# A second transformer block regrouped as 16 positions x 8 sequences, with its attention on TensorE, behind cross-attention as a phase of its own

## The chip, the cores and the metric

The kernel runs on one core of a Trainium2 chip. The metric is the device time of one execution in microseconds (us). Five engines work side by side, each on a queue of its own in program order: TensorE (PE, with its weight loads shown apart as PEld), VectorE (DVE), ScalarE (ACT), GpSimd (POOL) and SyncE (SP, which only issues DMAs here). They wait for each other through semaphores.

## The reference, cut to what matters

There are 8 sequences of 512 positions with 512 features: 4096 tokens. Cross-attention has 16 heads and reads 77 context rows for each sequence. The second block works **across the 8 sequences at one position**: its hidden states are (S=8, B=512, H=512), so a token attends to the at most 8 tokens with its own position in the sequences up to its own. It has 16 query heads and 4 key-value heads of 32 features.

```python
x = x + xattn(layernorm(x), ctx_1024, ctx_1024, ...)   # 16 heads, 77 keys, causal over (512, 77)
# second block, on layernorm(x) as (8, 512, 512)
ln1 = layer_norm(h, ln1_weight, ln1_bias); qkv = ln1 @ qkv_weight.T
scores = einsum('bgqsd,bgtd->bgqst', qb, kb) * scale   # s, t: the 8 sequences; b: the 512 positions
attn = softmax(where(tril(8, 8), scores, min)); ao = einsum('bgqst,bgtd->bgqsd', attn, vb)
h1 = h + ao @ proj_weight.T
logits = layer_norm(h1, ...) @ router_weight            # 8 experts, top 2, capacity 1280 each
out = x + h1 + moe(...)                                 # experts 512 -> 1024 -> 512, gelu
```

## The kernel before

The program has four parts, each a block of all engines with a barrier at its end: the setup (weights are loaded, two of them transposed on PE, all split into a high and a low half for three-pass products; keys `kT` and values `va` of the context are made), the main part, the routing, and the experts.

The main part handles 32 tiles of 128 tokens. Tile t holds 128 positions of sequence t % 8 (`row0`); chunk t // 8 says which 128 positions. It runs in 40 steps; in step i every stage works on its own tile, named by its lag: load and norm (0), `xt` transposes (1), `q` for two tiles at even steps (2), scores of cross-attention and softmax (2), `pt` transposes of the shares, `pv`, `wo` (3), residual, statistics, `zt` and `qkv` of the second block (4), its attention (5 and 6), `at` and `pj` (7), `z2t` and the router's logits `lg` (8). The lists are written out by hand for each engine, in one order that every step repeats. Four PSUM banks serve as a ring for all PE products in the order of `JOBS`; `bank_free` waits until the bank four jobs back has been read.

The attention of the second block before: POOL multiplies queries by the keys of the sequences so far (`prod_k`, L452) and shares by values (`prod_v`, L469), DVE sums both (L699, L710). Their size grows with the sequence number of the tile: 128 elements times (t % 8 + 1), four times each. So one step in eight is small and one in eight is large. The softmax of cross-attention reads PSUM: DVE adds the mask (L770, tiles under 8), takes the maximum (L773), ACT does 16 exponentials with accumulated sums (L626), DVE multiplies by the reciprocals (L690). `low_half` (L679) makes the low half of a split, for `xT`, `aT` and `oT`.

What PE waits for in one step, in its order: shares, `xT_lo` (q), the query evacuation (scores), `pT` (pv), `zT_lo` (qkv) and `oT_lo` (wo). `wo` comes last, behind 24 matmuls of `qkv`.

## Time and profile before

| | |
|---|---|
| median of 3 runs (lowest to highest) | 1815.31 us (1813.96 to 1817.59) |
| profiled execution, its own time | 1818.26 us |
| its span | 1816.5 us |
| mean granted TensorE clock, of full speed | 0.911 |
| setup, main part, routing, experts | 68, 912, 63, 774 us |

The four parts are read from the trace: the main part runs from 68 to 980 us of the span, the routing to 1043. The page gives busy shares of the whole span (PE 83%, DVE 61%, POOL 54%, ACT 44%), an average over parts with different limits.

### The profile page before, as it was taken

The numbers are of one execution on the slowest core, as the hardware profiler recorded it, in microseconds if no ns is written. First come the engines' busy times: TensorE is split into PE (matmuls) and PEld (weight loads), VectorE is DVE, ScalarE is ACT, GpSimd is POOL, SyncE is SP. The second block draws the span as 40 slices with busy tenths as digits, with TensorE's granted clock in tenths as the row PEclk, the third lists the DMA queues.
The fourth block names the chain that finished last, engine by engine and source line by source line (L and its number), as shares of the span: only waits on it lengthen the run. The fifth ranks groups of instructions, "written<-read, shape, count | busy, mean of one in ns | idle before, by whom it ended". The sixth has DMA issues, their size and how long they took to land. (4 is left out here: it accounts for less than half of the span.)

```text
span 1816.5 us, 31665 instructions
## 1 busy us (share of the span) xinstructions
PE 1513.9 (83%) x10604; PEld 1324.4 (73%) x10605; DVE 1105.9 (61%) x1778; ACT 802.6 (44%) x2385; POOL 975.8 (54%) x925
## 2 busy tenths in 40 slices
PE   7778877799777988789752579999999979999986
PEld 5367766677666776677642478989999968999975
DVE  3256888967897798877866953544333374353361
ACT  2066654565555655457421043544333354343240
POOL 2014676756785677667884254655344385454342
PEclk9879997899898988889875789999999989999999
DMA  7101101111101111111001132433333352433221
GB/s 188 35 18 36 44 28 36 36 49 48 47 24 47 49 36 36 36 36 42 24 35 71 45 109 64 94 95 101 74 71 81 58 128 66 92 94 88 34 37 21
DMA packets 57936, 106.95 MB, mean 59 GB/s; under 512 B 14314, under 2 KB 14314, under 8 KB 57771
## 3 DMA queue, kind: packets, MB, share of 16 engines
q1 hardware_dynamic: 26707, 58.42, 10.1%
q0 software_dynamic: 17920, 29.08, 9.4%
q10 hardware_dynamic: 13144, 17.23, 2.7%
q8 instruction: 106, 1.74, 0.4%
q14 instruction: 59, 0.48, 0.1%
HBM read 79.83 MB, written 37.75 MB: 65 GB/s over the span
## 5 line engine op out<-in xcount | busy, mean ns | idle before, releaser
L1347 PE MATMUL hidden_ps<-gT,w 128*128 128x256 f32 x2880 | 351.8, 284 | 5.4 <-ACT hT L1269 2.5
L1347 PEld LDWEIGHTS hidden_ps<-gT,w 128*128 128x128 f32 x2880 | 349.4, 192 | 9.1 <-ACT hT L1269 5.2
L1376 PE MATMUL expert_ps<-w,hT 128*128 128x512 f32 x1440 | 340.2, 396 | 8.0 <-DVE og L1316 8.0
L1376 PEld LDWEIGHTS expert_ps<-w,hT 128*128 128x128 f32 x1440 | 272.1, 191 | 64.7 <-DVE og L1316 8.5
L1294 DVE TENSOR_TENSOR hT<-gl,hT 128x512 fp32r<-128x512 f32 x160 | 132.0, 834 | 246.9 <-ACT hT L1269 238.8
L1156 POOL TENSOR_TENSOR w<-raw,w 128x1024 fp32r<-128x1024 f32 x64 | 155.3, 2442 | 206.5 <-ACT w L1150 205.6
L1267 ACT ACTIVATE gl<-hidden_ps 128x512 f32<-128x512 f32 x160 | 95.8, 598 | 335.1 <-PE hidden_ps L1347 239.2
L1249 POOL DMA_INDIRECT out_dram<-og,idx x80 | 132.7, 1659 | 155.0 <-DVE og L1316 141.3
L452 POOL TENSOR_TENSOR prod_k<-qb,kc 128x128 f32<-128x128 f32 (+7 forms) x128 | 182.6, 1428 | 30.4 <-ACT vs L652 28.1
L626 ACT ACTIVATE pr<-score_ps,nm 128x77 f32<-128x77 f32 x512 | 158.7, 363 | 78.1 <-DVE nm L776 78.1
L469 POOL TENSOR_TENSOR prod_v<-pa,vc 128x128 f32<-128x128 f32 (+7 forms) x128 | 156.5, 1233 | 24.7 <-DVE ao L710 20.5
L1316 DVE TENSOR_SCALAR og<-expert_ps,shares 128x512 f32<-128x512 f32 x80 | 59.1, 749 | 161.3 <-PE expert_ps L1376 150.8
L710 DVE TENSOR_REDUCE ao<-prod_v 128x128 f32<-128x128 f32 (+7 forms) x128 | 138.5, 1097 | 5.1 <-POOL prod_v L469 5.1
L699 DVE TENSOR_REDUCE sc<-prod_k 128x4 f32<-128x128 f32 (+7 forms) x128 | 95.7, 749 | 55.5 <-POOL prod_k L452 55.5
L1277 ACT ACTIVATE gT<-yk 128x256 fp32r<-128x256 f32 x160 | 67.2, 420 | 139.2 <-DVE yk L1303 135.6
L626 ACT ACTIVATION_READ_ACCUMULATOR pr<-score_ps,nm 128x1 f32 x512 | 125.0, 244 | 0.0
L840 PE MATMUL ring_ps<-ident,pr 128*77 128x128 f32 x512 | 88.1, 328 | 40.5 <-DVE pr L690 37.2
L823 PE MATMUL ring_ps<-ident,ao 128*128 128x128 f32 x128 | 28.4, 363 | 110.9 <-DVE x L724 83.5
L840 PEld LDWEIGHTS ring_ps<-ident,pr 128*77 128x77 f32 x512 | 75.9, 184 | 52.2 <-DVE pr L690 45.6
L1239 POOL DMA_INDIRECT xg<-normed_tokens,idx x80 | 86.7, 1084 | 49.3 <-POOL idx L1234 34.6
L823 PEld LDWEIGHTS ring_ps<-ident,ao 128*128 128x128 f32 x128 | 18.7, 181 | 117.6 <-DVE ao L710 111.1
L1269 ACT ACTIVATE hT<-hidden_ps 128x512 fp32r<-128x512 f32 x160 | 95.6, 598 | 14.8 <-PE expert_ps L1376 14.8
(186 smaller groups left out, 3352.7 us busy)
## 6 DMA issues: line engine op xcount, KB each, us to landing
raw<-L_ffn_moe_w_dram SPq DMA_DIRECT2D x64, 512.0 KB
xa<-x_dram SPq DMA_DIRECT2D x32, 256.0 KB, 2.8
xc<-x_dram SPq DMA_DIRECT2D x32, 256.0 KB, 2.7
out_dram<-x ACTq DMA_DIRECT2D x32, 256.0 KB, 2.0
normed_tokens<-z ACTq DMA_DIRECT2D x32, 256.0 KB, 2.3
xg<-normed_tokens,idx POOLq DMA_INDIRECT x80
out_dram<-og,idx POOLq DMA_INDIRECT x80
cx<-ctx_dram SPq DMA_DIRECT2D x1, 1232.0 KB
```

The costliest lines, as they stand in the source:

```text
L452: pool.tensor_tensor(prod_k[:, g % 2, 0:n * P].rearrange("p (t h d) -> p t h d", t=n, h=HQ), bc(qb[:, t.s % 2, g * P:(g + 1) * P].rearrang ...
L469: pool.tensor_tensor(prod_v[:, g % 2, 0:n * P].rearrange("p (t h d) -> p t h d", t=n, h=HQ), bc(w, 3, shape), bc(vc[:, 0:n, g * DH:(g + 1) ...
L626: e = act.activation(pr[:, b, g, :], psS[:, b, g * SK:(g + 1) * SK], ACT.Exp, bias=nm[:, h:h + 1], scale=SCALE, accum_out=den[:, h:h + 1])
L699: dve.tensor_reduce(sc[:, g * HQ:(g + 1) * HQ, 0:n].rearrange("p h t -> p t h"), prod_k[:, g % 2, 0:n * P].rearrange("p (t h d) -> p t h d ...
L710: dve.tensor_reduce(ao[:, g * P:(g + 1) * P], prod_v[:, g % 2, 0:n * P].rearrange("p (t f) -> p f t", t=n), X, ALU.add).then_inc(s["sums_v ...
L840: last = pe.transpose(bank(i, "pt", b)[0:SK, g * P:(g + 1) * P], pr[:, b, g, :], ident[:, :])
L1156: pool.tensor_tensor(weight_piece(p, 1, j), raw[:, j % 2, :], weight_piece(p, 0, j).bitcast(F32), ALU.subtract).then_inc(s["w_lo"], 1)
L1249: pool.indirect_dma_start(out=out2d[:, :], out_offset=rows(g, k), in_=og[:, k, :], in_offset=None, bounds_check=N - 1, oob_is_err=False, c ...
L1267: act.activation(gl[:, q % 2, :], pH[:, q, :], ACT.Gelu_apprx_tanh)
L1294: dve.tensor_tensor(o[1], gl[:, q % 2, :], o[0].bitcast(F32), ALU.subtract)\
L1347: last = pe.matmul(pH[:, q, f * W:(f + 1) * W], w1[p][l][:, k, cols], xT[g.s % 2][r][:, k, :], start=k == 0 and n == 0, stop=k == KT - 1 a ...
L1376: last = pe.matmul(pY[:, k, :], hT[par][l][:, f, k * P:(k + 1) * P], w2[p][r][:, f, :], start=f == 0 and n == 0, stop=f == FT - 1 and n == 2)
```

## The change

The main part is written anew. Cross-attention keeps its tiles and runs in steps 0 to about 36; its result is written to DRAM (`mid`). The second block reads `mid` back in tiles of another shape, 16 positions of all 8 sequences (`block_rows`: four DMAs of 32 rows, each row 2 KB), and its tile f works in steps 30 + f to 33 + f (`FF` = 30), so that the program has 66 steps in place of 40, written out without a loop. In a tile of the second block, each group of 32 tokens holds 4 positions x 8 sequences. Its attention is done on PE: scores by one matmul that adds the mask and four of 128x128 against a block-diagonal `kbd` (`s2`), four transposes of the shares (`p2t`), four matmuls against `vbd` (`o2`). DVE turns queries, keys and the result in blocks of 32x32 (`dve.transpose`). `prod_k`, `prod_v` and their sums are gone, the `at` transposes too.

In cross-attention, the 16 exponentials with accumulators become a subtraction of the maxima on DVE (2), two exponentials on ACT, two sums on DVE; the multiplication by the reciprocals goes from DVE to POOL, and `pt`, `pv` and `wo` come one step later (`LP` = 4). The residual is added at lag 5.

The weights and the context come from the host already laid out and transposed, and so do the constants, so the setup's PE transposes and POOL's constants are gone. The routing loads six constants by DMA and adds a third prefix product (`lower_seq`), since a tile's tokens are no longer in order. The experts are as before.

```diff
+TB = 32
+FX = 6
...
+    mid = nc.dram_tensor("attended_rows", [N, D], F32, kind="Internal").ap()
...
-JOBS = [("pt", 3, 0), ("pt", 3, 1), ("xt", 1, 0), ("at", 7, 0), ("pt", 3, 2), ("pt", 3, 3), ("q", 2, 0), ("q", 2, 1),
-        ("z2t", 8, 0), ("zt", 4, 0), ("pj", 7, 0), ("pv", 3, 0), ("lg", 8, 0), ("qkv", 4, 0), ("qkv", 4, 1),
-        ("wo", 3, 0)]
+LP = 4
+FF = NT - 2
+STEPS = NT + FF + 4
...
+def ring_jobs(i):
+    tx, tq, tp = tile(i, 1), tile(i, 2), tile(i, LP)
+    fz, fs, fo, fr = (tile(i, FF + n) for n in range(4))
+    jobs = [("pt", tp, 0), ("pt", tp, 1), ("xt", tx, 0), ("pt", tp, 2), ("pt", tp, 3), ("zt", fz, 0), ("o2", fo, 0)]
+    if i % 2 == 0:
+        jobs += [("q", tq, 0), ("q", tq, 1)]
+    jobs += [("s2", fs, 0), ("pv", tp, 0), ("z2t", fr, 0), ("pj", fo, 0), ("p2t", fs, 0), ("qkv", fz, 0),
+             ("lg", fr, 0), ("qkv", fz, 1), ("wo", tp, 0)]
+    return [job for job in jobs if job[1] is not None]
...
+        jobs = [("k", m, h) for m in range(KT) for h in range(2)] + [("v", b, 0) for b in range(S)]
...
+                    for n in range(2):
+                        sp.wait_ge(x2_out[n], 16 * 4 * (f // 8 + 1))
+                    need(sp, base_out[f % FX], 64 * (f // FX))
+                    for j in range(4):
+                        sp.dma_start(fx[TB * j:TB * (j + 1), f % FX, :], block_rows(mid, f, j))\
+                          .then_inc(fx_in[f % FX], 16)
...
-                    pool.tensor_tensor(prod_k[:, g % 2, 0:n * P].rearrange("p (t h d) -> p t h d", t=n, h=HQ),
-                                       bc(qb[:, t.s % 2, g * P:(g + 1) * P].rearrange("p (h d) -> p h d", h=HQ),
-                                          1, shape),
-                                       bc(kc[:, 0:n, g * DH:(g + 1) * DH], 2, shape), ALU.mult)\
-                        .then_inc(s["prods_k"], 1)
...
+                t = tile(i, LP - 1)
+                if t is not None:
+                    for half in range(2):
+                        pool.wait_ge(s["rec_done"], 2 * t + half + 1)
+                        shares = pr[:, t % 2, 2 * half:2 * half + 2, :, :].rearrange("p b g k -> p (b g) k")
+                        pool.tensor_tensor(shares, shares, bc(rec[:, t % 2, 8 * half:8 * half + 8], 2, [P, 8, SK]),
+                                           ALU.mult).then_inc(s["shared"], 1)
...
+                if f is not None:
+                    pool.wait_ge(s["rec2_done"], f + 1)
+                    pool.tensor_tensor(p2[:, f % 2, :, :], p2[:, f % 2, :, :], bc(rec2[:, f % 2, :], 2, [P, 16, TB]),
+                                       ALU.mult).then_inc(s["shared2"], 1)
...
+                f = tile(i, FF - 1)
+                if f is not None:
+                    pool.wait_ge(s["stat_f"], f + 1)
+                    var = mvf[:, f % 2, 1:2]
+                    link(pool, "pool_link", linked,
+                         pool.tensor_scalar(wf[:, 0:1], var, 1.0 + EPS, EPS * EPS, ALU.mult, ALU.add))
+                    pool.tensor_tensor(rff[:, f % 2:f % 2 + 1], wf[:, 0:1], expo[:, 0:1], ALU.pow)\
                         .then_inc(s["rstd_f"], 1)
...
+                    need(pool, s["h0_done"], f - 3)
+                    link(pool, "pool_link", linked, power(rf[:, f % 4:f % 4 + 1], var, wf[:, 1:2]))
+                    pool.tensor_scalar(shift[:, f % 4:f % 4 + 1], mvf[:, f % 2, 0:1], rf[:, f % 4:f % 4 + 1], -1.0,
+                                       ALU.mult, ALU.mult).then_inc(s["shift_f"], 1)
+                f = tile(i, FF + 2)
+                if f is not None:
+                    pool.wait_ge(s["stat_h"], f + 1)
+                    power(rh[:, f % 2:f % 2 + 1], mvh[:, f % 2, 1:2], wh[:, :]).then_inc(s["rstd_h"], 1)
+                    pool.tensor_tensor(fx[:, f % FX, :], fx[:, f % FX, :], h1[:, f % 2, :], ALU.add)\
                         .then_inc(s["base_done"], 1)
...
-                                               bias=nm[:, h:h + 1], scale=SCALE, accum_out=den[:, h:h + 1])
-                        e.then_inc(s["exp_done"], 1)
-                t = At(c, i - 5)
...
+                if t is not None:
+                    for half in range(2):
+                        act.wait_ge(s["shifted"], 2 * t + half + 1)
+                        shares = pr[:, t % 2, 2 * half:2 * half + 2, :, :]
+                        act.activation(shares, shares, ACT.Exp, scale=SCALE).then_inc(s["exp_done"], 1)
...
+                f = tile(i, FF + 1)
+                if f is not None:
+                    dve.wait_ge(s["qkv_mm"], 2 * f + 1)
+                    need(dve, s["s2_mm"], f)
+                    dve.transpose(hq[:, :, :], parts(bank("qkv", f, 0))).then_inc(s["q_turned"], 1)
+                    dve.wait_ge(s["v_kept"], f + 1)
+                    for j in range(4):
+                        rows = slice(TB * j, TB * (j + 1))
+                        k_turn = dve.transpose(kbd[rows, :, j, :],
+                                               bank("qkv", f, 1)[rows, 0:P].rearrange("p (g d) -> p g d", g=NKV))
+                    k_turn.then_inc(s["k_turned"], 1)
...
+                if f is not None:
+                    dve.wait_ge(s["o2_mm"], f + 1)
+                    need(dve, s["a_lo"], f)
+                    dve.transpose(ao[:, :], bank("o2", f)).then_inc(s["ao_done"], 1)
...
+                    dve.wait_ge(s["a_hi"], f + 1)
+                    dve.tensor_tensor(aT[1][:, :, :], parts(ao[:, :]), aT[0][:, :, :].bitcast(F32),
+                                      ALU.subtract).then_inc(s["a_lo"], 1)
...
+                    dve.wait_ge(s["s2_mm"], f + 1)
+                    scores = bank("s2", f).rearrange("p (b k) -> p b k", b=16)
+                    need(dve, s["p2t_mm"], f - 1)
+                    chained(dve.tensor_reduce(nm2[:, :], scores, X, ALU.max, negate=True))
+                    dve.tensor_tensor(p2[:, f % 2, :, :], scores, bc(nm2[:, :], 2, [P, 16, TB]), ALU.add)\
+                       .then_inc(s["s2_sub"], 1)
...
+                    chained(dve.tensor_reduce(nm[:, :].rearrange("p (b g) -> p b g", b=4), scores, X, ALU.max,
+                                              negate=True))
+                    need(dve, s["pt_mm"], 4 * (t - 1))
+                    for half in range(2):
+                        dve.tensor_tensor(pr[:, t % 2, 2 * half:2 * half + 2, :, :],
+                                          scores[:, 2 * half:2 * half + 2, :, :],
+                                          bc(nm[:, 8 * half:8 * half + 8].rearrange("p (b g) -> p b g", b=2), 3,
+                                             [P, 2, 4, SK]), ALU.add).then_inc(s["shifted"], 1)
...
+                    dve.wait_ge(s["o_hi"], t + 1)
+                    dve.tensor_tensor(oT[1][:, :, :], parts(bank("pv", t)), oT[0][:, :, :].bitcast(F32),
+                                      ALU.subtract).then_inc(s["o_lo"], 1)
...
+                    dve.wait_ge(s["exp2"], f + 1)
+                    need(dve, s["shared2"], f - 1)
+                    chained(dve.tensor_reduce(den2[:, :], p2[:, f % 2, :, :], X, ALU.add))
+                    dve.reciprocal(rec2[:, f % 2, :], den2[:, :]).then_inc(s["rec2_done"], 1)
...
+                    dve.wait_ge(s["h0_done"], f + 1)
+                    dve.wait_ge(s["pj_mm"], f + 1)
+                    dve.tensor_tensor(h1[:, f % 2, :], bank("pj", f), h1[:, f % 2, :], ALU.add)\
+                       .then_inc(s["h1_done"], 1)
+                    dve.wait_ge(s["h1_done"], f + 1)
+                    stats(h1[:, f % 2, :], bnh, mvh[:, f % 2, :]).then_inc(s["stat_h"], 1)
...
+                    dve.wait_ge(fx_in[f % FX], 64 * (f // FX + 1))
+                    need(dve, s["shift_f"], f - 1)
+                    stats(fx[:, f % FX, :], bnf, mvf[:, f % 2, :]).then_inc(s["stat_f"], 1)
...
+                    for half in range(2):
+                        heads = slice(8 * half, 8 * half + 8)
+                        dve.wait_ge(s["exp_done"], 2 * t + half + 1)
+                        shares = pr[:, t % 2, 2 * half:2 * half + 2, :, :].rearrange("p b g k -> p (b g) k")
+                        chained(dve.tensor_reduce(den[:, heads], shares, X, ALU.add))
...
+                    dve.wait_ge(s["rstd_h"], f + 1)
+                    need(dve, z2_out[f % 2], 64 * (f // 2))
+                    need(dve, s["z2t_mm"], f - 1)
+                    dve.tensor_scalar(z2[:, f % 2, :], h1[:, f % 2, :], mvh[:, f % 2, 0:1], rh[:, f % 2:f % 2 + 1],
+                                      ALU.subtract, ALU.mult).then_inc(s["z2_done"], 1)
...
+                    dve.wait_ge(s["rstd_f"], f + 1)
+                    need(dve, s["zt_mm"], f)
+                    dve.tensor_scalar(z[:, :], fx[:, f % FX, :], mvf[:, f % 2, 0:1], rff[:, f % 2:f % 2 + 1],
...
+                if tp is not None:
+                    turn_shares(tp, (0, 1))
+                if tx is not None:
+                    pe.wait_ge(s["normed_x"], tx + 1)
+                    transposes("xt", tx, xa[:, tx % 3, :]).then_inc(s["xt_mm"], 1)
+                if tp is not None:
+                    turn_shares(tp, (2, 3))
+                if fz is not None:
+                    pe.wait_ge(s["z_done"], fz + 1)
+                    transposes("zt", fz, z[:, :]).then_inc(s["zt_mm"], 1)
+                if fo is not None:
+                    pe.wait_ge(s["p2t_evac"], fo + 1)
+                    pe.wait_ge(s["v_spread"], fo + 1)
+                    bank_free(pe, "o2", fo)
+                    for g in range(NKV):
+                        last = pe.matmul(bank("o2", fo)[:, g * P:(g + 1) * P], p2T[:, g, :],
+                                         vbd[:, fo % 2, g, :, :].rearrange("p j d -> p (j d)"), start=True, stop=True)
+                    last.then_inc(s["o2_mm"], 1)
...
+                if fs is not None:
+                    pe.wait_ge(s["q_turned"], fs + 1)
+                    pe.wait_ge(s["k_turned"], fs + 1)
+                    bank_free(pe, "s2", fs)
+                    pe.matmul(bank("s2", fs), token_sel[:, :], token_mask[:, :], start=True, stop=False)
+                    for g in range(NKV):
+                        last = pe.matmul(bank("s2", fs)[:, g * P:(g + 1) * P], hq[:, g, :],
+                                         kbd[:, g, :, :].rearrange("p j k -> p (j k)"),
+                                         start=False, stop=g == NKV - 1)
+                    last.then_inc(s["s2_mm"], 1)
+                if tq is not None:
+                    pe.wait_ge(s["q_evac"], 4 * (tq // 2) + 4)
...
+                if tp is not None:
+                    pe.wait_ge(s["pt_evac"], 4 * tp + 4)
...
+                if fr is not None:
+                    pe.wait_ge(s["z2_done"], fr + 1)
+                    transposes("z2t", fr, z2[:, fr % 2, :]).then_inc(s["z2t_mm"], 1)
+                if fo is not None:
+                    pe.wait_ge(s["a_lo"], fo + 1)
+                    bank_free(pe, "pj", fo)
+                    split_matmuls(pe, bank("pj", fo), lambda h, k: aT[h][:, k, :], lambda h, k: wpj[h][:, k, :])\
+                        .then_inc(s["pj_mm"], 1)
+                if fs is not None:
+                    pe.wait_ge(s["shared2"], fs + 1)
...
+                if fz is not None:
+                    pe.wait_ge(s["z_lo"], fz + 1)
+                    bank_free(pe, "qkv", fz, 0)
+                if fr is not None:
+                    pe.wait_ge(s["y2_done"], 4 * fr + 4)
+                    bank_free(pe, "lg", fr)
...
+                if tp is not None:
+                    pe.wait_ge(s["o_lo"], tp + 1)
+                    bank_free(pe, "wo", tp)
+                    split_matmuls(pe, bank("wo", tp), lambda h, k: oT[h][:, k, :], lambda h, k: wo[h][:, k, :])\
                         .then_inc(s["wo_mm"], 1)
...
+            for dst, name in ((ranks, "expert_ranks"), (ahead, "ahead_in_tile"), (same_seq, "same_seq"),
+                              (lower_seq, "lower_seq"), (ramp, "ramp"), (number, "token_numbers")):
+                sp.dma_start(dst[:, :], a[name]).then_inc(made, 16)
...
+            dve.tensor_reduce(lower[:, :], pp[:, 2, 0:NT * E].rearrange("p (t e) -> p e t", e=E), X, ALU.add)
...
+            pe.matmul(pp[:, 2, 0:NT * E], lower_seq[:, :], flat, start=True, stop=True).then_inc(prefixed, 1)
```

## Rows read from the trace of the kernel before

**Rows 1.** The windows view: stretch, length, busy by engine, PEclk, DMA share, GB/s.

```profile
97.80:112.60 14.80, 11.87 (x97) 10.03 (x98) 8.43 (x14) 9.80 (x48) 2.03 (x3) 0.62 0.06 19
...
588.74:607.45 18.71, 18.09 (x200) 15.43 (x204) 15.31 (x34) 15.54 (x59) 13.02 (x21) 1.00 0.25 87
716.21:748.30 32.09, 24.94 (x141) 22.25 (x144) 27.65 (x34) 14.22 (x54) 21.92 (x21) 0.84 0.05 18
68.00:980.00 912.00, 710.84 (x5632) 613.39 (x5632) 696.24 (x1070) 492.14 (x1824) 577.73 (x640) 0.87 0.11 38
```

**Rows 2.** The waits of PE, 470 to 800 us: total, times, longest.

```profile
PE ring_ps L823 <- DVE x L724: 42.5, 11, 5.2
```

**Rows 3.** The timeline of step 3, an odd step without the second block.

```profile
97.80 1.99 PE L840 MATMUL ring_ps<-ident,pr 128*77 128x128 f32 x8 [6.94 <-DVE pr L690]
...
102.28 1.13 PE L869 MATMUL score_ps<-kT,qT 32*128 32x77 f32 x32
...
103.34 1.08 PE L880 MATMUL ring_ps<-pT,va 77*32 77x128 f32 x32
...
104.96 1.44 DVE L773 TENSOR_REDUCE nm<-score_ps 128x16 f32<-128x1232 f32 x1
...
106.52 0.68 DVE L679 TENSOR_TENSOR oT_lo<-ring_ps,oT_hi 128x512 fp32r<-128x512 f32 x1
...
107.35 0.77 PE L413 MATMUL ring_ps<-wo_hi,oT_hi 128*128 128x512 f32 x1 [2.93 <-DVE oT_lo L679]
...
112.56 1.03 PE L840 MATMUL ring_ps<-ident,pr 128*77 128x128 f32 x8
```

**Rows 4.** The timeline of steps 4 and 5 on PE: q's ends, wo, scores, shares.

```profile
115.63 0.36 PE L413 MATMUL ring_ps<-xT_hi,wq_hi 128*128 128x256 f32 x1 [0.62 <-DVE xT_lo L679]
...
121.28 0.28 PE L413 MATMUL ring_ps<-xT_hi,wq_lo 128*128 128x256 f32 x1
...
122.49 1.13 PE L869 MATMUL score_ps<-kT,qT 32*128 32x77 f32 x32 [0.49 <-ACT qT L577]
...
131.76 0.39 PE L413 MATMUL ring_ps<-wo_hi,oT_hi 128*128 128x512 f32 x1
...
134.50 1.03 PE L840 MATMUL ring_ps<-ident,pr 128*77 128x128 f32 x8
```

**Rows 5.** Groups of instructions by form, 470 to 800 us: total busy, mean ns.

```profile
L690 DVE TENSOR_TENSOR pr<-pr,rec 128x616 f32<-128x616 f32 x24 | 33.5, 1398 | 0.8
...
L593 ACT ACTIVATE y<-ring_ps,ln1b,ln1w 128x128 f32<-128x128 f32 x48 | 18.2, 464 | 1.7 <-PE ring_ps L823 1.5
...
L509 POOL TENSOR_TENSOR zT_lo<-y,zT_hi 128x512 fp32r<-128x512 f32 x12 | 15.3, 1274 | 22.6 <-ACT zT_hi L598 22.6
...
L806 DVE TENSOR_SCALAR z<-h,mvf,rf 128x512 f32<-128x512 f32 x12 | 14.7, 1229 | 0.0
...
L469 POOL TENSOR_TENSOR prod_v<-pa,vc 128x640 f32<-128x640 f32 x8 | 10.7, 1355 | 0.3 <-DVE ao L710 0.3
...
L724 DVE TENSOR_TENSOR x<-ring_ps,xc 128x512 f32<-128x512 f32 x12 | 8.2, 681 | 2.5 <-issue 2.4
...
L598 ACT ACTIVATE zT_hi<-y 128x512 fp32r<-128x512 f32 x12 | 7.6, 633 | 0.5
L441 POOL TENSOR_TENSOR rc<-wc,expo 128x1 f32<-128x1 f32 x12 | 7.4, 619 | 1.0
```

**Rows 6.** The timeline of the setup.

```profile
15.40 19.26 PE L294 MATMUL setup_ps<-cT,rk 128*128 128x308 f32 x64 [0.66 <-DVE cT L260]
...
34.50 1.91 PE L309 MATMUL setup_ps<-ident,rpj 128*128 128x128 f32 x16
...
36.24 2.95 PE L309 MATMUL setup_ps<-ident,rqkv 128*128 128x128 f32 x24
...
67.08 0.69 DVE L268 TENSOR_TENSOR va<-setup_ps,bv 77x512 f32<-77x512 f32 x1 [2.75 <-PE setup_ps L299]
```

**Rows 7.** DMA issues: bytes of one, us from issue to landing.

```profile
xa<-x_dram SPq DMA_DIRECT2D x32, 256.0 KB, 2.8
```

More of the change, by code:

```diff
@@ L435, in _, with power @@
+            for f in range(NT - FX, NT):
+                sp.wait_ge(base_out[f % FX], 64 * (f // FX + 1))
+            for f in range(NT - 2, NT):
+                sp.wait_ge(z2_out[f % 2], 64 * (f // 2 + 1))
         @block.gpsimd
         def _(pool):
-            def rstd(dst, var, work, chain, count):
-                pool.tensor_scalar(work, var, EPS, None, ALU.add).then_inc(chain, 1)
-                need(pool, chain, count)
+            linked = [0]
+            def power(dst, var, work):
+                link(pool, "pool_link", linked, pool.tensor_scalar(work, var, EPS, None, ALU.add))
@@ L520, in step @@
[L520 to L532 removed]
+                f = tile(i, FF + 1)
@@ new lines, in _ @@
+                f = tile(i, FF + 1)
+                if f is not None:
+                    act.wait_ge(s["p2t_mm"], f + 1)
+                    need(act, s["o2_mm"], f)
+                    act.activation(p2T[:, :, :], parts(bank("p2t", f)), ACT.Copy).then_inc(s["p2t_evac"], 1)
+                f = tile(i, FF + 3)
+                if f is not None:
+                    act.wait_ge(s["lg_mm"], f + 1)
+                    act.activation(logits[:, f, :], bank("lg", f)[:, 0:E], ACT.Copy).then_inc(s["lg_evac"], 1)
@@ L1035, in _ @@
                                    pp[:, 1, 0:NT * E].rearrange("p (t e) -> p t e", e=E), ALU.subtract))
+            link(dve.tensor_tensor(place[:, :, :], place[:, :, :], bc(lower[:, :], 1, shape), ALU.add))
             for k in range(2):
```

923 lines of the change are left out of this document (369 added, 554 removed), and 3 rows, old and new, of the table read_out.

## The prediction, made blind

> **What bounds the kernel now.** I read the windows of the four parts first, then the waits of PE in the middle of the main part, then the timeline of single steps. The main part takes 912 us, 28.5 for each of its 32 tiles, with PE busy for 711 us, DVE for 696 and POOL for 578, at a granted clock of 0.87 [rows 1]. The reader should compare two steps there. The stretch from 588.74 to 607.45 us, from one residual of the second block to the next, is 18.7 us long with PE busy for 18.1 at full clock: where the attention products are short, PE sets the step. The stretch from 716.21 is 32.1 us long, with DVE busy for 27.7 and PE for 24.9: where they are long, DVE and POOL set it. PE then waits, above all for DVE's residual (42.5 us in 11 waits) [rows 2]. So the bound changes with the tile, and the sums leave some 200 us of the main part in which PE does nothing.
>
> **PE's own work after the change.** At full clock 48 q matmuls start in 5.65 + 0.12 = 5.8 us, once for two tiles [rows 4], and 12 matmuls of 512 columns (wo) take 134.50 - 131.76 = 2.75 us, 0.23 each [rows 4]; pj takes the same. qkv is 12 of these and 12 of 256 columns: 2.75 + 1.4 = 4.2. Eight transposes end 1.03 after they start and take about 0.9 of PE [rows 4], so 16 share transposes cost 1.8 and a group of four 0.45. Scores and pv take 1.05 each [rows 3]. Cross-attention is thus 1.8 + 0.45 + 2.9 + 1.05 + 1.05 + 2.75 = 10.0 us for a tile (12.9 at even steps, 7.1 at odd ones). New are true fp32 matmuls of 128 columns: the trace shows such matmuls only at 308 columns, 32 of them in 19.3 us (64 records), which gives 0.25 for 128 [rows 6]; a transpose at 0.11 is the bound below. I take 0.22. s2 is then 4 x 0.22 + 0.23 = 1.1, o2 0.9, p2t 0.45, and a tile of the second block 0.45 (zt) + 0.9 + 1.1 + 0.45 (z2t) + 2.75 + 0.45 + 4.2 + 0.9 (lg, eight short records between the others) = 11.2. Together 21.2 us; before, the same list with at and without s2, o2 and p2t was 19.3. PE gains 2 us of work for a tile.
>
> **What is removed.** POOL's products and DVE's sums go entirely, and with them the long steps. On ACT 16 exponentials with accumulator reads go for two of 616 elements. DVE gives the 616-element multiplications, 1.40 us each on average [rows 5], to POOL (about 1.35, as for 640 elements [rows 5]) and gets two subtractions from PSUM. A subtraction of 616 elements is bounded by 0.68 for 512 and 1.44 for 1232 [rows 3]: 0.8. DVE's residual, which also reads one PSUM and one SBUF operand, has a mean of 0.68 beside a busy POOL [rows 5], so I don't charge the 1.40. The Trainium skill (GPSIMD Engine Reference, section 1, Specifications) says that POOL shares its SBUF interface with DVE instructions that have two SBUF inputs; that agrees with 0.68 against 1.40, and without it the two subtractions would cost 1.2 us more.
>
> No engine but PE has 21 us of work for a tile any more: DVE has some 18, POOL 13. But the two phases no longer lie on top of each other, and each then has only its own work to put into its waits.
>
> **The cross-attention phase.** Take the end of wo as zero. PE does shares and xt to 2.2. At an even step q starts at 3.1 (q's start after the shares is late by 0.62 for `xT_lo` [rows 4]) and ends at 8.8; the query evacuation puts the scores at 9.9 (1.1 after q [rows 4]) to 10.9. Now DVE's order counts: maximum 1.44, two subtractions 1.6, and only then `oT_lo` 0.68 [rows 3], with waits 4.0 in all. pv is done at 12.0, and nothing of the second block is left to put between pv and wo. wo starts at 14.8 after 2.9 of idling. Step 3 of before has just this form: wo waited 2.93 us for `oT_lo` and then took 112.56 - 107.35 = 5.2 us in place of 2.75, at the lower level of the clock (0.62 over that step) [rows 1, 3]. So the even step ends at 19.9. At an odd step the scores come right after the shares but behind DVE's norm, at 3.7; `pT` and pv are done at 4.7, `oT_lo` at 7.3, wo at 12.3. The mean is 16.1 us for 10.0 of work. As a test, step 3, odd and with the mask, took 112.56 - 97.80 = 14.8 [rows 3]; my odd step is 12.3 + 1.5 for the mask = 13.8, and step 3's cold shares and its lack of subtractions nearly cancel. With a warm wo it is 17.5 and 9.9, mean 13.7. POOL's multiplications are made a step ahead and hide.
>
> **The second phase.** Take DVE's last norm `z` as zero; DVE turns queries until 0.7 and keys until 1.7, zt and o2 run beside that, and s2 ends at 2.8. A 32x32 turn on DVE is not in the trace; I bound it by 0.54 and 0.8 for 512 elements and take 0.7 as for a copy from PSUM, and four key turns at 0.2 to 0.3. ACT: y four times 0.38 to 0.46, the high half 0.63 [rows 5], then `aT`'s high half at 2.9 to 3.5; DVE's `a_lo` at 4.25; pj 4.3 to 7.1. DVE goes from `a_lo` to maximum and subtraction (5.7), ACT's exponential (6.4), sum and reciprocal (7.3), POOL's multiplication (1.27 for 512 [rows 5], 8.65), p2t, and qkv with lg from 9.2 to 14.3. Beside this runs the other chain: pj, DVE's h1 and two statistics (9.9), POOL's five small operations and two more, of which three powers at 0.6 [rows 5], to 13.0, DVE's z2 and z. z2 meets POOL's add of 1.27 and costs 1.23 on average, against 0.53 alone [rows 5]. That chain closes at 15.1. PE is idle 4 of 15 us, in gaps of about 1 and 1.6. If pj runs at the lower clock (2.4 more) the chain closes at 17.2, with qkv too at 17.5. I take 16.2 for 11.2 of work. The DMAs hide: SP's 12 issues and the landing (2.8 [rows 7]) take about 8 us and are wanted a step later; uncovered they would be those 8 us once in each step.
>
> The Trainium skill (TensorE: Matmul & The Clock Gate, section HAM oscillation) says that a loop whose every turn has a wait on PE starts each turn's work at half clock. By that rule both phases cost their upper values, and the whole would be near 1970; the trace agrees for wo in step 3, and the middle value of the second phase doubts it.
>
> **The sum**, against the 912 us: first steps up to step 4, 30 (97.80 - 68.00 before [rows 1, 3]); steps 4 to 29, 26 x 16.1 = 419; the mask at six of them, 1.5 each, 9; steps 30 to 35 with both blocks, 21.2 of PE when full, less at their start, with 2 to 3 of waiting, 131; steps 36 to 61, 26 x 16.2 = 421; the last four and the stores, 27. Together 1037, +125. Setup: two groups of transposes, 1.9 + 2.95 [rows 6], and some 2 of context transposes that the loads don't cover go, -7; its end, v's matmuls, stays. Routing: six small loads at 2.8 and their issues [rows 7], one more product, one more link: +5. The experts stay. 1818.3 - 7 + 125 + 5 = 1941 for an execution like the profiled one, which lay 3 us above the median: **1938 us**. With its own bounds (16.1 to 13.7, 16.2 to 15.1 or 17.5, fp32 matmuls and turns at either end, overlap 125 to 146): 1841 to 1990.
>
> **The rivals.** (1) The clock stays up through waits of 1.5 to 3 us: 13.7 and 15.1, 26 x 2.4 + 26 x 1.1 + 6 less, 1841; up to 1880 if half of them do. For it: waits of 0.6 in step 4 left q fast [rows 4]. Against: step 3. Chance 0.20. (2) Faster: the waits for `oT_lo` and `shared2` are filled, because DVE is idle in both phases and PE's sum sets the steps. Both together 21.2 for a tile in place of 32.3, 26 x 11.1 = 289 less, near 1650. It decides below 912 + 2 - 197 = 717 us for the 26 pairs, 27.6 a pair: 4.7 of the 11.1 us of waiting would have to be absent. For it: before, with long lists, PE reached 18.1 of 18.7. Against: the waits are made by the order of DVE's list, not by its load. Chance 0.10 for anything faster. (3) Turns on DVE cost double or the overlap jams: 2 us more in 26 steps and 20 more, above 1990. Chance 0.08. (4) No difference, 0.02. My forecast has 0.60.
>
> 0.2% is about what a measurement of this kernel can tell from no change. Faster 0.10, same 0.02, slower 0.88. The range 1830 to 1990 leaves out the faster cases and (3).
>
> **What would show it.** A main part of about 1040 us with 66 steps; in steps 10 to 28 PE's largest wait at wo for `oT_lo`, near 2.9 and 2.6 us, then 12 matmuls at the lower clock; in steps 36 to 61 waits at pj and p2t, a step of 15 to 17.5 us, PE busy 70 to 75%. The prediction is wrong if wo starts right behind pv, or if these steps are shorter than 13 us.

## The result and the profile after

The changed kernel is slower: 1971.09 us (1969.05 to 1971.91, 4 runs) against 1816.45 us (1813.96 to 1817.73) on the same chip, a ratio of 1.0851 [1.0833, 1.087], or +154.6 us. The forecast was 1938 us, +123, in a range of 1830 to 1990.

The windows view of the kernel after, with the columns of [rows 1]. The first two stretches are an even and an odd step of cross-attention alone, from one end of `wo` to the next; the third is a step with both blocks, the fourth a step of the second block alone; then the whole main part, and two long stretches in which only one block runs.

```profile
393.40:413.10 19.70, 15.46 (x146) 13.57 (x145) 8.76 (x13) 6.22 (x12) 4.43 (x5) 0.83 0.12 41
413.10:426.10 13.00, 9.69 (x98) 7.94 (x97) 8.65 (x13) 4.54 (x8) 4.42 (x5) 0.74 0.20 62
565.00:592.50 27.50, 25.27 (x207) 21.98 (x206) 17.71 (x29) 10.96 (x22) 11.09 (x14) 0.94 0.09 29
849.70:868.00 18.30, 15.58 (x80) 13.34 (x80) 10.52 (x19) 6.58 (x16) 7.00 (x11) 0.82 0.13 43
56.40:1128.94 1072.54, 832.81 (x6176) 700.89 (x6176) 628.94 (x1000) 378.83 (x800) 373.88 (x513) 0.86 0.14 48
100.00:480.00 380.00, 285.67 (x2754) 245.75 (x2753) 205.32 (x303) 122.94 (x229) 99.90 (x113) 0.81 0.14 47
720.00:1050.00 330.00, 265.59 (x1414) 217.91 (x1412) 207.64 (x343) 123.89 (x287) 141.10 (x218) 0.91 0.14 46
```

POOL went from 578 busy microseconds in the main part [rows 1] to 374, as the change has it. Yet the main part grew from 912.0 to 1072.5 us, because a tile now passes through two kinds of step, 16.2 and 17.1 us on average, where it had one of 28.5.

The waits of PE in the two long stretches (total, times, longest), which take the place of [rows 2]; the first three rows are of 100 to 480 us, the others of 720 to 1050:

```profile
PE ring_ps L366 <- DVE oT_lo L652: 76.3, 23, 4.8
PE score_ps L759 <- ACT qT L523: 11.1, 12, 0.9
PE ring_ps L366 <- DVE xT_lo L609: 6.9, 11, 0.6
...
PE ring_ps L701 <- DVE z L693: 38.9, 19, 3.0
PE ring_ps L783 <- POOL p L455: 13.9, 13, 1.1
PE ring_ps L366 <- DVE aT_lo L624: 9.4, 13, 1.0
```

Now the timeline of the end of the even step above (start, duration, engine, line), which answers to [rows 3]:

```profile
403.32 1.13 PE L759 MATMUL score_ps<-kT,qT 32*128 32x77 f32 x32 [0.93 <-ACT qT L523]
...
404.38 1.08 PE L768 MATMUL ring_ps<-pT,va 77*32 77x128 f32 x32
404.52 1.44 DVE L641 TENSOR_REDUCE nm<-score_ps 128x16 f32<-128x1232 f32 x1 [6.91 <-PE score_ps L759]
405.53 0.60 ACT L541 ACTIVATE oT_hi<-ring_ps 128x512 fp32r<-128x512 f32 x1 [2.26 <-PE ring_ps L768]
405.99 1.50 DVE L645 TENSOR_TENSOR pr<-score_ps,nm 128x616 f32<-128x616 f32 x2
...
407.42 0.68 DVE L652 TENSOR_TENSOR oT_lo<-ring_ps,oT_hi 128x512 fp32r<-128x512 f32 x1
...
408.15 0.80 PE L366 MATMUL ring_ps<-wo_hi,oT_hi 128*128 128x512 f32 x1 [2.69 <-DVE oT_lo L652]
...
413.08 0.60 PE L709 MATMUL ring_ps<-ident,pr 128*77 128x128 f32 x4
```

`oT_lo` needs nothing but `oT_hi`, which ACT has made by 406.13. It starts at 407.42, behind the two subtractions of the softmax. Then the 12 matmuls of `wo` take 413.08 - 408.15 = 4.9 us, not the 2.75 of [rows 4].

The timeline of a step of the second block alone, from POOL's power operation for `rh` to `pj`:

```profile
860.35 0.57 POOL L422 TENSOR_TENSOR rh<-wh,expo 128x1 f32<-128x1 f32 x1
...
860.87 1.27 POOL L477 TENSOR_TENSOR fx<-fx,h 128x512 f32<-128x512 f32 x1
860.95 1.48 DVE L687 TENSOR_SCALAR z<-h,mvh,rh 128x512 f32<-128x512 f32 x1 [3.23 <-POOL rh L422]
...
862.09 1.23 POOL L442 TENSOR_TENSOR vbd<-vn,blocks 128x512 f32<-128x512 f32 x1
862.35 1.26 DVE L693 TENSOR_SCALAR z<-fx,mvf,rff 128x512 f32<-128x512 f32 x1
...
863.52 0.70 DVE L587 STREAM_TRANSPOSE hq<-ring_ps 128x512 f32<-128x512 f32 x1
863.66 1.11 PE L701 MATMUL ring_ps<-ident,z 128*128 128x128 f32 x4 [2.65 <-DVE z L693]
864.16 1.25 DVE L591 STREAM_TRANSPOSE kbd<-ring_ps 32x128 f32<-32x128 f32 x4
...
868.92 0.50 PE L366 MATMUL ring_ps<-wpj_hi,aT_hi 128*128 128x512 f32 x1 [0.42 <-DVE aT_lo L624]
```

Read the two norms `z` (L687 is `z2`, L693 the first norm of the tile that comes next) against POOL's two operations. POOL's end at 862.14 and 863.32, the norms at 862.43 and 863.61: each norm ends 0.29 us after the POOL operation beside it. The input of L693 has long been there, its `rff` came at 858.6; it stands behind `z2` in DVE's list, and `z2` waits for `rh`. PE stands still for 2.65 us.

Outside the steps, these rows of the setup's timeline and of the DMA issues answer to [rows 6, 7]:

```profile
8.97 18.95 PE L272 MATMUL setup_ps<-cT,rk 128*128 128x308 f32 x64 [8.97 <-DMA rk<-wk_rows_dram]
27.76 27.63 PE L277 MATMUL setup_ps<-rv,cT 128*77 128x512 f32 x64
...
xa<-x_dram SPq DMA_DIRECT2D x32, 256.0 KB, 2.7
```

The keys' products start at 8.97 us in place of 15.40, and the main part at 56.40 in place of 68.05. So +153.3 us of span (1969.8 - 1816.5) are -11.7 for the setup, +160.5 for the main part and +4.5 for what follows (routing 3.4, experts 1.1).

### The profile page after: what moved, and what is told of

Its sections match the earlier page's. It is cut to its first block and busy times, and to the rows that moved or that the text cites. A ratio compares the mean times of both kernels' runs of the same rounds, so it can differ in the third digit from the quotient of the medians.

```text
span 1969.8 us, 30370 instructions
## 1 busy us (share of the span) xinstructions
PE 1626.7 (83%) x11078; PEld 1403.7 (71%) x11079; DVE 1031.4 (52%) x1692; ACT 689.0 (35%) x1353; POOL 768.3 (39%) x785
## 5 line engine op out<-in xcount | busy, mean ns | idle before, releaser
L431 POOL TENSOR_TENSOR pr<-pr,rec 128x616 f32<-128x616 f32 x64 | 77.2, 1227 | 243.2 <-DVE rec L681 243.2
L366 PE MATMUL ring_ps<-wo_hi,oT_hi 128*128 128x512 f32 x128 | 76.7, 599 | 85.4 <-DVE oT_lo L652 85.4
L486 ACT ACTIVATE pT<-ring_ps 77x512 f32<-77x512 f32 x128 | 68.6, 593 | 159.1 <-PE ring_ps L709 159.1
L366 PEld LDWEIGHTS ring_ps<-wo_hi,oT_hi 128*128 128x128 f32 x128 | 36.8, 287 | 100.3 <-DVE oT_lo L652 92.4
L1158 ACT ACTIVATE hT<-hidden_ps 128x512 fp32r<-128x512 f32 x160 | 95.5, 597 | 14.6 <-PE expert_ps L1265 14.6
L687 DVE TENSOR_SCALAR z<-h,mvh,rh 128x512 f32<-128x512 f32 x32 | 47.7, 1489 | 93.2 <-POOL rh L422 93.2
L701 PE MATMUL ring_ps<-ident,z 128*128 128x128 f32 x256 | 47.0, 314 | 55.0 <-DVE z L693 51.6
L1192 DVE TENSOR_SCALAR yk<-gather_ps,ln2w,ln2b 128x256 f32<-128x256 f32 x160 | 83.1, 540 | 11.0 <-PE gather_ps L1249 8.1
L641 DVE TENSOR_REDUCE nm<-score_ps 128x16 f32<-128x1232 f32 x32 | 45.9, 1436 | 77.6 <-PE score_ps L759 77.3
L455 POOL TENSOR_TENSOR p<-p,rec 128x512 f32<-128x512 f32 x32 | 33.5, 1047 | 134.8 <-DVE rec L659 134.8
L450 POOL TENSOR_TENSOR zT_lo<-y,zT_hi 128x512 fp32r<-128x512 f32 x32 | 40.8, 1275 | 115.7 <-ACT zT_hi L511 115.7
```

Of the source, the lines that this page charges most:

```text
L366: last = pe.matmul(dst, lhs(l, k), rhs(r, k), start=k == 0 and n == 0, stop=k == KT - 1 and n == 2)
L431: pool.tensor_tensor(shares, shares, bc(rec[:, t % 2, 8 * half:8 * half + 8], 2, [P, 8, SK]), ALU.mult).then_inc(s["shared"], 1)
L486: act.activation(pT[:, j, :, :], bank("pt", t, j)[0:SK, :].rearrange("p (g n) -> p g n", g=4), ACT.Copy).then_inc(s["pt_evac"], 1)
L1158: act.activation(hT[g.s % 2][0][:, 2 * q:2 * q + 2, :].rearrange("p f n -> p (f n)"), pH[:, q, :], ACT.Gelu_apprx_tanh).then_inc(s["gelu"], 1)
L1192: dve.tensor_scalar(yk[:, k % 2, :].rearrange("p (b n) -> p b n", b=GB), pT[:, :, k * P:(k + 1) * P], ln2w[:, k:k + 1], ln2b[:, k:k + 1], ...
```

## The experiments

Beside these runs, the kernel before measured 1816.15, 1814.38, 1816.46 and 1813.82 us, with experiments 1 to 4, 5 to 8, 9 to 11, and 12 in turn. A ratio is always to before. Spacings of steps are taken between successive residuals `x2` or successive `aT_lo` in each trace.

**1. `oT_lo` ahead of the subtractions.** It stands on DVE right behind the maximum; nothing else moves.

```diff
@@ DVE, behind the maximum of a tile of cross-attention
+                low_half_of_o(tile(i, LP))
                 if t is not None:
                     need(dve, s["pt_mm"], 4 * (t - 1))
...
-                t = tile(i, LP)
-                if t is not None:
-                    dve.wait_ge(s["o_hi"], t + 1)
-                    dve.tensor_tensor(oT[1][:, :, :], ...
```

> Edit: on VectorE the low half of oT is made right behind the maximum of the scores, ahead of the two subtractions, in place of behind them. Theory (the wait at wo is made by the order of VectorE's list): wo starts some 2.6 us after the scores in place of 4.0, in each of 32 steps, 32 x 1.5 = 46 us less; if the shorter wait also leaves the clock at its upper level for wo, up to 2.4 us more in each, 115 less in all: 1855 to 1925 us. Rival (the phases are bound by the sum of an engine's work or by something behind wo): no change, 1971.

Measured: 1933.79 us, ratio 1.0644 [1.062, 1.0668], 37 us less. The wait and the window of 100 to 480 us:

```profile
PE ring_ps L366 <- DVE oT_lo L584: 49.5, 25, 3.4
```

```profile
100.00:480.00 380.00, 310.05 (x3062) 266.68 (x3060) 227.38 (x332) 135.90 (x253) 110.57 (x125) 0.84 0.16 53
```

The wait went from 3.3 to 2.0 us each, and a step from 16.2 to 14.7. The order of DVE's list makes this part of the wait; the other 2.0 us stay. The granted clock rose only from 0.81 to 0.84, so what the lower clock costs is still there, and the gain is below what was expected.

**2. The second block 16 steps behind in place of 30** (`FF = 16`), so that 16 steps and not two have both blocks in full.

> Edit: FF = 16 in place of 30, nothing else; 52 steps, 20 of them with both blocks. Theory (each phase alone has nothing to put into its waits; a pair of steps apart costs 16.2 + 17.1 = 33.3 us, a step with both about 23): 14 pairs more lie on top of each other, 14 x 10.3 = 144 us less, 1827 us (1805 to 1860). Rival (the time is lost by the new form of the attention itself: its matmuls, turns and round trip through DRAM): it costs the same wherever it lies, within 20 us of 1971.

Measured: 1855.43 us, ratio 1.0218 [1.0198, 1.0238], 116 us less. A step with both takes 25.3 us, against 16.2 + 17.1 = 33.3 for two apart. One step less of lag thus saves 33.3 - 25.3 = 8.0 us, 14 of them 112. The expectation had a full step at 23; in its place PE waits 29.2 us in 13 waits of 350 to 680 us for POOL's `p`, the shares `p2` (2.2 each).

**3. `z` ahead of `z2` on DVE.**

```diff
@@ DVE, end of a step
+                f = tile(i, FF - 1)
+                if f is not None:
+                    dve.wait_ge(s["rstd_f"], f + 1)
...
+                    dve.tensor_scalar(z[:, :], fx[:, f % FX, :], ...).then_inc(s["z_done"], 1)
                 f = tile(i, FF + 2)
                 if f is not None:
                     dve.wait_ge(s["rstd_h"], f + 1)
...
-                f = tile(i, FF - 1)
-                if f is not None:
-                    dve.wait_ge(s["rstd_f"], f + 1)
...
-                    dve.tensor_scalar(z[:, :], fx[:, f % FX, :], ...).then_inc(s["z_done"], 1)
```

> Edit: at the end of VectorE's step the norm z of the next tile comes ahead of z2. Theory (in the second phase the chain through GpSimd's small operations and VectorE's two norms, each held by a GpSimd add or multiplication beside it, starts the next step late; PE waits 2.05 us a step for z): z comes some 3 us earlier, the turns behind z2 about 1 us earlier: 1.0 us in 30 steps, 1940 us (1925 to 1960). Rival (the chain of pj, softmax and qkv on PE sets the step, z is merely the wait that shows): within 5 us of 1971.

Measured: 1909.22 us, ratio 1.0512 [1.0492, 1.0532], 62 us less, twice what was expected. The window, the waits of PE and the two norms by form, 720 to 1050 us:

```profile
720.00:1050.00 330.00, 278.24 (x1639) 227.46 (x1638) 221.14 (x404) 146.42 (x336) 163.27 (x240) 1.00 0.15 53
```

```profile
PE ring_ps L783 <- POOL p L455: 24.6, 23, 1.1
PE ring_ps L731 <- DVE hq L587: 20.5, 21, 1.1
```

```profile
L693 DVE TENSOR_SCALAR z<-h,mvh,rh 128x512 f32<-128x512 f32 x23 | 34.4, 1497 | 42.0 <-POOL rh L422 42.0
L686 DVE TENSOR_SCALAR z<-fx,mvf,rff 128x512 f32<-128x512 f32 x21 | 11.6, 551 | 19.9 <-POOL rff L467 19.9
```

The step went from 17.1 to 14.6 us and the granted clock from 0.91 to 1.00. The norm `z` (`z<-fx`, L686 here and L693 in the changed kernel) fell from 1.32 us on average to 0.55: it now lies in DVE's wait for `rh`, when POOL has only operations of one element a partition to do. `z2` (`z<-h`) still costs 1.50. The order cost 26 x 2.5 = 65 us in all. Three things went with it, and no run tells them apart: the norm's wait for `rh`, its longer time beside POOL, and the lower clock.

**4. PE's wait filled.** While PE waits for `oT_lo` in a step without the second block, it does 11 useless matmuls of 128 columns into the bank that `wo` then overwrites. They add work and nothing that anyone needs.

```diff
                 if tp is not None:
-                    pe.wait_ge(s["o_lo"], tp + 1)
                     bank_free(pe, "wo", tp)
+                    if fz is None:
+                        for n in range(11):
+                            pe.matmul(bank("wo", tp)[:, 0:P], ident, ident, ...)
+                    pe.wait_ge(s["o_lo"], tp + 1)
```

> Edit: while PE waits for oT's low half in steps without the second block, it multiplies the identity by itself 11 times (2.5 us) into the bank that wo then overwrites. This adds work without use. Theory (the wait costs twice: its own 2.7 us, and wo's 12 matmuls at the lower level of the clock, 5.1 in place of 2.75): the wait stays, the clock stays up, 26 to 28 steps x 2.3 = 62 us less, 1909 us (1895 to 1930). Rival (the lower clock at wo has another cause): no change, or some us more.

Measured: 1920.68 us, ratio 1.0578 [1.0551, 1.0606], 50 us less, with everything of the change in place. The window shows what the clock did:

```profile
100.00:480.00 380.00, 343.63 (x3693) 309.02 (x3692) 235.55 (x347) 141.98 (x265) 115.99 (x135) 0.98 0.17 56
```

The granted clock is 0.98 where it was 0.81, and a step takes 14.3 us in place of 16.2. The useless matmuls hand no data to anyone, so these 2 us a step come from the clock.

**5 and 6. The edits together**: 1 and 3 with the lag left at 30, then all three.

> Edit: oT's low half right behind the maximum and z ahead of z2, together, with FF = 30 as in the changed kernel. Theory (the two waits lie in different phases and are made by the order of VectorE's list): the two gains add, 1971 - 37 - 62 = 1872 us (1865 to 1882), and the kernel stays slower than the one before, since the phases still lie apart. Rival (both edits mend one common cause, such as the clock): less than the sum, 1895 or more.

> Edit: both orders of before and FF = 16. Theory: a step with both blocks is 25.4 us as with FF = 16 alone, and only the 16 steps of each phase that stay alone gain, 1.4 and 2.3 us each: 1855 - 18 - 33 = 1804 us (1795 to 1820), about as fast as the kernel before. Rival (in a step with both blocks the early wait for oT's high half holds VectorE up): 1820 to 1850.

Measured: 1869.95 us, ratio 1.0305 [1.0275, 1.0335], and 1808.14 us, ratio 0.9957 [0.9942, 0.9972]. The first says that even with both orders mended the phases one behind the other lose: 14.61 + 14.55 = 29.2 us for a tile, against 28.5 before. The second is the first version below before, by 0.4%. The lag now saves less, 29.2 - 25.2 = 4.0 us a step, 14 of them 56 (measured 62). The three gains do not add up: a step with both blocks takes 25.3 us in experiment 2 and 25.2 here, so there the two orders gain next to nothing. The waits that 1 and 3 shorten are filled in it by the other block's work.

**7. The softmax of cross-attention as before the change**: 16 exponentials a tile on ACT, with the maximum as bias and collected sums, in place of two subtractions and two sums on DVE. Only this part is undone; the second block stays 30 steps behind.

```diff
@@ DVE
-                    for half in range(2):
-                        dve.tensor_tensor(pr[...], scores[...], bc(nm[...]), ALU.add)
+                    dve.tensor_scalar(nm[:, :], nm[:, :], -SCALE, None, ALU.mult)
...
-                        chained(dve.tensor_reduce(den[:, heads], shares, X, ALU.add))
@@ ACT
-                        act.activation(shares, shares, ACT.Exp, scale=SCALE)
+                        for b in range(2 * half, 2 * half + 2):
+                            for g in range(4):
+                                act.activation(pr[...], psS[...], ACT.Exp, bias=nm[...], scale=SCALE, accum_out=den[...])
```

> Edit: the softmax of cross-attention as before the change (16 exponentials with accumulated sums on ScalarE, no subtractions and no sums on VectorE), all else as in the changed kernel. Theory (what lies on the path is VectorE between the scores and oT's low half): the two subtractions, 1.6 us, go and a small operation of 0.2 comes, so wo starts 1.2 us earlier in 32 steps; ScalarE's 5 us for a tile hide: 1933 us (1920 to 1945). Rival (this part of the change is its gain, since ScalarE is relieved): slower than 1971, 1985 or more.

Measured: 1933.89 us, ratio 1.0651 [1.0623, 1.0679], 37 us less and the same as experiment 1: `oT_lo` now has no subtractions ahead of it. PE's wait for it is 51.8 us in 25, and a step 14.8. So in this phase the subtractions cost what they delay, and no more than that shows, though ACT has 16 exponentials again. It is not so in a step with both blocks, as experiment 10 shows.

**8. The transposes `p2t` behind `qkv`**, on top of 6, to fill PE's wait for `p`: PE goes on with `qkv` and turns the shares later, ahead of `wo`; ACT's copy of the result goes to the end of its list.

> Edit: as the kernel with both orders and FF = 16, and the transposes of the second block's shares come behind qkv on PE in place of ahead of it, with their evacuation last on ScalarE. Theory (PE waits 2.2 us in a step with both blocks, and about 1 in one of the second phase, for GpSimd's multiplication of the shares, and 24 matmuls that don't need it stand behind): 20 x 2.2 + 16 x 0.8 = 57 us less than its neighbour, near 1750 us (1735 to 1785). Rival (VectorE's list or the ring of banks is the next bound): within 15 us of its neighbour.

Measured: 1852.63 us, ratio 1.0205 [1.0178, 1.0232]: 44 us more than 6 where 58 less were expected. The wait for `p` is gone from these steps, but PE's timeline has another, here in a step with both blocks:

```profile
466.17 0.60 PE L808 MATMUL ring_ps<-ident,p 128*128 128x128 f32 x4
470.50 0.76 PE L366 MATMUL ring_ps<-wo_hi,oT_hi 128*128 128x512 f32 x1 [3.73 <-DVE hq L593]
```

And its waits of 350 to 680 us say that this is every step:

```profile
PE ring_ps L366 <- DVE hq L593: 38.7, 12, 3.7
```

`wo` reads no `hq`. It waits for its bank. The ring has four banks, so each product waits until the bank of the product four places ahead has been read. In the order `pj, p2t, qkv, lg, qkv, wo` the fourth ahead of `wo` is `p2t`, read early by ACT. In `pj, qkv, lg, qkv, p2t, wo` it is the first half of `qkv`, which `hq` reads, behind `z2` and thus behind POOL's `rh`.

**9 to 11. The same transposes behind `wo`**, where the bank of `wo` is the one that `pj` had (experiment 9); then the kernel of experiment 6 with the softmax of experiment 7 and the transposes where the change put them (10); then both edits (11). The cut shows the order of 9 and 11.

```diff
-    jobs += [..., ("pj", fo, 0), ("p2t", fs, 0), ("qkv", fz, 0), ("lg", fr, 0), ("qkv", fz, 1), ("wo", tp, 0)]
+    jobs += [..., ("pj", fo, 0), ("qkv", fz, 0), ("lg", fr, 0), ("qkv", fz, 1), ("wo", tp, 0), ("p2t", fs, 0)]
```

> The version with oT_lo early, z ahead of z2 and the second block 16 steps behind (1808.1 us), with the transposes of the shares p2 moved to the very end of the step, behind wo. The run with these transposes ahead of wo came out at 1852.6 us instead of 1750: its trace shows TensorE waiting 38.7 us in 12 times in 350:680, 3.2 us a time, at wo for hq, the turned queries. The ring has four banks, and the move made the bank of wo that of the first half of qkv, which hq sets free only behind z2 and POOL's rh. Theory (the bank was the cause): behind wo, the transposes leave wo the bank that pj had, which is long free; the wait for p (2.2 us in a step with both blocks, 1.2 us in one of the second block alone) goes, some 17 x 2.2 + 13 x 1.2 = 53 us: 1755 us. Rival (POOL's way to z2 and hq sets the step, wherever the transposes stand): full steps stay at 25 us or become 27, 1808 to 1850 us.

> The version of 1808.1 us with the softmax of cross-attention as it was before the change: 16 exponentials a tile on ACT read the scores themselves, with the maximum as bias and the sums collected by ACT, and VectorE does no subtractions and no sums. Theory (VectorE's queue ahead of rec2 feeds the wait for p in the steps with both blocks): 1.50 us of subtractions go from in front of the sums of the second block, and 1.5 us of sums from in front of z; full steps go from 25.4 to about 24, steps of cross-attention alone stay at 14.7, 1785 us. Rival (ACT's 16 short exponentials, some 5 us against 1.4, hold up p2 and vn instead): no gain or a loss of 1 us a full step, 1808 to 1825 us.

> Both edits together, the transposes of p2 behind wo and the softmax of cross-attention as it was before the change. If their gains are of different waits: 1755 - 23 = 1732 us. If the wait for p is what both of them take away: as the transposes behind wo alone, 1755 us.

Measured: 1798.71 us, ratio 0.9901 [0.9884, 0.9917]; 1789.62 us, ratio 0.9854 [0.9837, 0.9871]; 1796.08 us, ratio 0.9887 [0.9869, 0.9906]. The theory of the bank holds for the steps with both blocks: 24.0 us each, against 25.2 in 6 and 27.3 in 8. Yet 9 gains 9 us where 53 were expected. In the steps with both, the transposes themselves now stand four places behind the first half of `qkv` and wait for `hq`, 12.6 us in 14 waits from 350 to 680 us. And the theory misses the other phase. Without cross-attention there is no `wo` in the ring, and the transposes behind `qkv` move the banks again: the steps of the second block alone take 15.9 us in place of 14.5, with these waits of PE from 760 to 960 us in experiment 9:

```profile
PE ring_ps L704 <- DVE hq L593: 17.8, 10, 1.8
PE ring_ps L366 <- DVE aT_lo L630: 14.7, 12, 1.4
```

The older softmax alone (10) comes near its expected 1785 us and gives 23.4 us for a step with both. Both edits give 23.3, no less, and bring the 15.9 with them; so most of the two gains is of one wait, as the second case of the last expectation had it, though its 1755 us did not come, and the total is worse than in 10. What holds now is seen in the window of 350 to 680 us of experiment 11:

```profile
350.00:680.00 330.00, 321.17 (x2784) 272.27 (x2783) 213.90 (x390) 215.14 (x776) 165.64 (x222) 1.00 0.20 67
```

PE is busy for 321 of 330 us at full clock, 22.6 us of each 23.3: here the sum of PE's work sets the step.

**12. The place by phase.** `p2t` stands behind `wo` while there is one and where the change put it when there is none; the lag is 14.

> Both edits of the version of 1796.1 us (softmax as before the change, transposes of p2 behind wo), but in the steps without cross-attention the transposes stand again where the change put them, ahead of qkv; and the second block runs 14 steps behind instead of 16. Theory (where p2's transposes stand decides through the ring of four banks, and behind wo is right only while there is a wo): the steps of the second block alone go from 15.9 back to 14.5 us, 13 x 1.4 = 18 us; each step less of lag trades a step of either part alone, 14.7 + 14.5 us, for one with both, 23.25 us, two of them 12 us: 1766 us. Rival (the 15.9 us are not of the transposes' place): 1784 us by the lag alone, with the steps of the second block still at 15.9.

Measured: 1764.74 us (1763.61 to 1765.3, 5 runs), ratio 0.9727 [0.9709, 0.9745], 1.3 us from what was expected. Two windows, of steps with both blocks and of the second block alone:

```profile
350.00:680.00 330.00, 321.01 (x2764) 272.12 (x2761) 216.05 (x396) 216.00 (x781) 165.19 (x223) 1.00 0.20 67
769.00:886.00 117.00, 99.73 (x589) 81.59 (x589) 78.54 (x146) 53.05 (x122) 58.07 (x88) 1.00 0.16 53
```

The steps of the second block are 14.5 us long again and those with both 23.3. This version beats both kernels, by 49 us the one before and by 206 the changed one, with the same matrix form of attention.

## Why the prediction was right, and where it was off

The direction, the mechanism and the range held. The terms of its sum, one by one, with the ends of the steps as read from the trace:

| term | forecast | measured |
|---|---|---|
| setup | -7 | -11.7 |
| first steps, to the end of step 4 | 46 | 58.6 |
| steps 5 to 29 with the mask | 411 | 408.3 |
| steps 30 to 35 | 131 | 134.8 |
| steps 36 to 61 | 421 | 441.4 |
| last four and stores | 27 | 29.4 |
| routing and experts | +5 | +4.5 |

(The forecast's 30 for the steps ahead of step 4 and its 16.1 for step 4 make the 46 of the second row; 25 steps and the mask's 9 make the 411. Step 4 is an even one with the mask, so the forecast's own terms give it 19.9 + 1.5 = 21.4; the third row has the same 5.3 us too much.)

**The step of cross-attention** was right: 19.7 to 20.1 and 12.0 to 13.1 us alternate, a mean of 16.2 for 16.1. Behind the tiles with the mask, `wo` waits 2.7 us at even steps and 3.1 to 3.3 at odd ones, for 2.9 and 2.6. Both of its causes were put to the test. A part of the wait for `oT_lo` is made by DVE's order (experiments 1 and 7: 1.5 us a step), and the lower clock of `wo` by PE's wait (experiment 4: 2.0 us a step). The filled form also answers rival 1, that the clock stays up through such waits: it doesn't, and with a clock that does a step is 14.3 us, near the 13.7 that the rival was given. The Trainium skill (TensorE: Matmul & The Clock Gate, section HAM oscillation) describes a loop of matmuls whose wait in every turn lets the next turn start at half clock. The trace agrees in cross-attention, 0.81 against 0.98 with the waits filled. In the second phase it agrees in part: at 0.91 the clock was down for some of the steps, and with 1.1 us waits left it was 1.00 (experiment 3). The 1970 that the prediction worked out by that rule is the time that came, but in part by luck, through other terms: 12.5 us are of the first steps, and in the second phase the order of two norms on DVE made the long wait; with that order changed, the lower clock went too.

**Steps 36 to 61** are the term that was mis-sized most, 17.0 us each for 16.2, +20.4. The failing step is "z2 meets POOL's add of 1.27 and costs 1.23 on average, against 0.53 alone": it priced one norm as held, and both are, 1.49 and 1.32 on average for 1.23 and 0.53, together 1.05 us more. It also took the order of `z2` and `z` for given, where experiment 3 shows that it decides 2.5 us of the step. The norms have one tensor input, and the trace shows them held all the same; `h`, with one operand from PSUM, took 0.63 us in experiment 8 (from 462.49 us) while POOL's `p` ran from 462.65. The prediction named only DVE instructions with two SBUF inputs. The sentence of the Trainium skill (GPSIMD Engine Reference, section 1, Specifications) has a second half: DVE instructions in a 2-port performance mode contend as well. The trace has no field for the mode, so no run here shows it; the norms beside POOL, each ending 0.29 us after it, would fit that half.

**The first steps** are +12.5 us. The 30 us were read from before's steps 0 to 2, and here four steps stand ahead of the first shares, since `LP` = 4. They took less all the same, and step 4 took 30.8 us where the sum had 16.1:

```profile
56.40:84.00 27.60, 13.79 (x124) 12.29 (x124) 11.99 (x20) 4.78 (x9) 4.21 (x9) 0.65 0.25 76
84.00:114.80 30.80, 20.44 (x145) 17.54 (x146) 17.14 (x25) 7.53 (x14) 8.66 (x10) 0.61 0.06 18
```

Of the 14.7 us too little, 5.3 are the even step and the mask, as said under the table. The rest lies in a step with a granted clock of 0.61, with a wait of 3.7 us for ACT's copy of the shares and one of 4.2 for `oT_lo`; no run takes them apart. The sum gave the first full turn the price of a middle one.

**The overlap** came as +3.8; its full steps are 27.5 and 23.4, where POOL's shares `p` end last (9.6 us in 4 waits). **The setup** was worth 4.7 more than forecast. The keys' products start 6.4 us earlier, and the forecast had 2 of that, for the context's transposes. The rest is that the key weights land earlier: at 8.97 us, where before they were issued at 1.31 and took 11.8.

**PE's own work** was priced too low: 21.2 us for a tile, where PE is busy for 22.6 of the 23.3 us of experiment 11, and 11.2 for the second block, where it is busy for 12.4 of the 14.5 us of experiment 12. The same shows in the sign "PE busy 70 to 75%" for steps 36 to 61, which came as 80%. It moved the forecast little, because waits and not PE's sum set these steps.

**Rival 2**, that the waits are filled and the kernel faster, had its point of decision at 27.6 us a pair. The changed kernel has 33.3; with both orders mended it has 29.2 and is still 3% slower (experiment 5). So the place of the second block decides as well, and not the two orders alone: apart, the phases lie above the limit, and only on top of each other (25.2, then 23.3 us) do they come below it. Its argument, that work of the other block fills waits as before, was right; that two blocks apart could do so was not.

What stays open: which part of the 0.2 to 1.1 us waits at `hq`, `p` and `aT_lo` in the 14.5 us step could be taken away; no run tried it. The lag was not tried below 14.

## What to carry to other kernels

Before two kinds of work are put one behind the other to shorten each engine's list, work out the step of each alone: the sum of waits along its chain, not the load of its engines. Here two phases, whose work on PE the prediction summed to 10 and 11 us, took 16 and 17, while laid together 23.3 us held all of it. Where an engine stands still in every step, look first at what is ahead of the awaited instruction in the releasing engine's list (two exchanges of order gave 101 us here), and before moving a product in a ring of buffers, count which reader frees the buffer it will land in.

## What was not expected of the hardware

- Useless matmuls in PE's wait made the kernel 50 us faster with nothing else changed: the granted clock rose from 0.81 to 0.98 between 100 and 480 us, and a step fell from 16.2 to 14.3 us.
- A norm of 512 elements on DVE, SBUF to SBUF with one tensor input, took 0.55 us when POOL had only single-element work, and 1.26 to 1.50 beside a POOL operation of 512 elements; it ended 0.29 us after POOL's did.
- DVE's block transposes: 0.70 us for 128x512 from PSUM (`hq`), as a copy of this size, and 1.25 us for the four of 32x128 (`kbd`), 0.3 each; the prediction had 0.7 and 0.2 to 0.3.
